# Node degrees and first edges of a graph kernel: a search in the sorted target list in place of one-hot counts

## The reference

```
x = x + attention_gnn(layernorm(x), edge_attr, src, dst, ...)   # softmax over the edges of one target
x = x + gated_experts(layernorm(x), ...)
x = x + mean_gnn(layernorm(x), src, dst, ...)                   # sums / max(degree, 1)
x = x + routed_experts(layernorm(x), ...)

# in attention_gnn:
ft = (feat @ W_fc).reshape(N, 8, 32);  eh, et = <ft, attn_h>, <ft, attn_t>     # per node and head
ee = <(edge_attr @ W_e), attn_e>                                               # per edge and head
e = leaky_relu(eh[src] + ee + et[dst])
a = softmax of e over the edges with the same dst
rst = segment_sum(ft[src] * a, dst)
```

## Time and profile before

| | us |
|---|---|
| three runs, median (lowest to highest) | 3279.69 (3274.05 to 3285.43) |
| the profiled execution | 3277.21 |
| its span | 3275.7 |
| PE busy | 2385.6 (73%) |
| DVE busy | 1885.0 (58%) |
| POOL busy | 1795.3 (55%) |
| ACT busy | 1315.9 (40%) |

### The profile page before, as it was taken

The page is one execution under the profiler, slowest core; times in us unless marked ns, Lnnn a source line. Parts: engine busy times, 40 slices in busy tenths (PEclk is TensorE's granted clock), DMA queues, the critical chain, the costliest instruction groups (busy, mean ns, idle before and its releaser), DMA issues. The chain is left out here.

```text
span 3275.7 us, 49346 instructions
## 1 busy us (share of the span) xinstructions
PE 2385.6 (73%) x12682; PEld 1986.9 (61%) x12682; DVE 1885.0 (58%) x5767; ACT 1315.9 (40%) x4659; POOL 1795.3 (55%) x1886
## 2 busy tenths in 40 slices
PE   5995366667666665657899698888888888746088
PEld 4884256666666565446677576666666666635077
DVE  7981388888889887657455433333333333366245
ACT  2332255555555544523445333333333333355033
POOL 0007777777777777041000677777777777250645
PEclk9998778887888877778999656656565566757589
DMA  7336644444444445460000333333333333321342
GB/s 209 100 109 149 201 110 112 113 112 112 112 111 114 112 112 153 139 185 26 23 16 19 113 106 105 107 105 106 105 106 105 106 105 106 113 62 34 97 139 86
DMA packets 264113, 348.42 MB, mean 106 GB/s; under 512 B 153632, under 2 KB 193686, under 8 KB 262331
## 3 DMA queue, kind: packets, MB, share of 16 engines
q0 software_dynamic: 87936, 235.05, 25.3%
q1 hardware_dynamic: 175908, 110.32, 13.1%
HBM read 288.25 MB, written 61.20 MB: 107 GB/s over the span
## 5 line engine op out<-in xcount | busy, mean ns | idle before, releaser
L1384 POOL DMA_INDIRECT Gb<-normed_rows,SRCT x784 | 741.3, 946 | 519.6 <-SPq L1376 281.0
L1405 PE MATMUL pAb<-HOTb,Gb 128*128 128x128 f32 x3136 | 845.5, 426 | 149.4 <-DMA Gb<-normed_rows,SRCT 117.5
L1405 PEld LDWEIGHTS pAb<-HOTb,Gb 128*128 128x128 f32 x3136 | 659.6, 297 | 335.4 <-DMA Gb<-normed_rows,SRCT 274.7
L1445 DVE TENSOR_TENSOR ACC<-ACC,pAb 128x256 f32 x784 | 330.8, 422 | 641.8 <-PE pAb L1405 569.1
L975 POOL DMA_INDIRECT GX<-ft_rows,SRCT x432 | 413.3, 957 | 131.8 <-issue 128.6
L1064 ACT ACTIVATE ACC<-apA 128x254 f32 x784 | 300.4, 383 | 413.5 <-PE apA L1137 339.4
L1137 PE MATMUL apA<-AHOT,GX 128*128 128x129 f32 x1920 | 306.2, 330 | 81.1 <-DVE GX L1286 80.8
L1137 PEld LDWEIGHTS apA<-AHOT,GX 128*128 128x128 f32 x1920 | 292.2, 243 | 98.8 <-DVE GX L1286 98.6
L1424 ACT ACTIVATE HOTb<-OFFb 128x1024 f32<-128x1024 f32 x98 | 103.6, 1057 | 604.8 <-PE pAb L1405 604.7
L975 POOL DMA_INDIRECT G<-ft_rows,SRCT x288 | 273.8, 951 | 87.6 <-issue 87.1
L1420 ACT ACTIVATE OFFb<-iota,NRELb 128x128 f32<-128x128 f32 x784 | 239.6, 388 | 6.7
(11 more groups left out here) (381 smaller groups left out, 4182.4 us busy)
## 6 DMA issues: line engine op xcount, KB each, us to landing
ebuf<-in_edge_attr_dram SPq DMA_DIRECT2D x49, 448.0 KB
Gb<-normed_rows,SRCT POOLq DMA_INDIRECT x784, 2.7
rows_by_expert<-ffn_PADT SPq DMA_DIRECT2D x1, 10360.0 KB, 42.3
sT<-rows_by_expert SPq DMA_DIRECT2D x80, 129.5 KB, 2.1
GX<-ft_rows,SRCT POOLq DMA_INDIRECT x480
sums_by_rank<-rrowa SPq DMA_DIRECT2D x49, 128.0 KB, 1.7
sums_by_rank<-rrowb SPq DMA_DIRECT2D x49, 128.0 KB, 1.7
GX<-in_x_dram SPq DMA_DIRECT2D x11, 560.0 KB
```

What stands on the lines that cost most here:

```text
L1384: pool.indirect_dma_start(G[g % R][m][:, :], None, TABLE[:, :], bass.IndirectOffsetOnAxis(ap=SRCT[:, t:t + 1], axis=0)).then_inc(g_in[g % ...
L1405: last = nc.tensor.matmul(pA[b][:, o:o + EP], G[k][m][:, c * 128:(c + 1) * 128], HOT[k % 2][:, m, :], start=True, stop=True)
L1445: last = nc.vector.tensor_tensor(acc[:, :, ds(b, EP)], acc[:, :, ds(b, EP)], pA[q][:, o:o + KD * EP].rearrange("p (c r) -> p c r", c=KD), ...
```

## The change

Instead of counting all edges, the new kernel searches. `dst` is cut into 3,125 rows of 32 edges, and 25 rows belong to each of 125 partitions (800 edges, the segment). For each of the 6,251 numbers v = 50p + i (one more than the nodes) it seeks the first edge whose target is not below v.

- First level: with the first target of each segment (`SX`) and of the next one (`SNX`), `segment_hits` marks on VectorE for each v the one segment in which it falls, in four batches of 13, 13, 13 and 12 values of i. `segments` multiplies each 125 x 125 mark matrix on TensorE with `SEG`, whose columns hold the first targets of the 25 rows of each segment and the number of its first row. `segment_rows` counts the rows that start below v and so finds v's row.
- Second level: GpSimd gathers for each i the row of 32 targets of all p, 51 indirect DMAs of 128 rows with 128 bytes, and `first_edges` counts the targets below v. The first edge is 32 times the row plus that count, and a degree is the difference of two neighbours.

The batches stand in groups 1 to 4 of the loop (hits up to two batches ahead); the four passes over all targets at the start, the `count` blocks, the transposition and the scan and prefix of degrees are gone. The last steps move: the cast `DX` goes behind the loop, `FIRSTI` no longer needs the prefix product, `CONT` is built after the last projection, and SP issues edge blocks 46 to 48 ahead of the load of `F`, which now also waits for `rq_ready`. SP gets three more DMAs at the start, GpSimd five more short instructions. The core of the diff:

```diff
-        HS = 4
-        FB = F[:, :].bitcast(bf16)
-        hotA = [...]
+        NV = NT + 1
+        SB = 13
+        SW = [min(SB, NV - b * SB) for b in range((NV + SB - 1) // SB)]
+        BW = 32
+        BK = E // BW // P
...
@@ sync
                 load_x(0)
+                ds32 = dst.rearrange("(p j) -> p j", j=BK * BW)
+                for a in PARTS:
+                    sp.dma_start(DVI[a, :], ds32[a, :]).then_inc(dv_in, 16)
+                sp.dma_start(SNI[0:P - 1, :], ds32[1:P, 0:1], allow_slow_non_contiguous=True).then_inc(dv_in, 16)
...
-                for c in range(n + 3, NCH - 3):
+                for c in range(n + 3, NCH):
                     load(c)
+                sp.wait_ge(rq_ready, 1)
                 sp.wait_ge(st, 16 * NT)
                 sp.dma_start(F[:, :], STARTD.rearrange("(p j) h -> p (j h)", j=ES)).then_inc(f_in, 16)
-                for c in range(NCH - 3, NCH):
-                    load(c)
@@ gpsimd
                 nc.gpsimd.memset(ETS[:, :], 0.0).then_inc(ets_zero, 1)
+                nc.gpsimd.memset(SEG[:, :], 0.0).then_inc(node_set, 1)
+                nc.gpsimd.iota(NODE.rearrange("p (i q) -> p i q", q=P), pattern=[[1, SB], [NT, P]], ...)
+                nc.gpsimd.iota(NODEV[:, :], pattern=[[1, NV]], base=0, channel_multiplier=NT, ...)
+                nc.gpsimd.memset(ROWI[:, :], 0).then_inc(node_set, 1)
+                nc.gpsimd.iota(SEG[:, BK:BK + 1], pattern=[[0, 1]], base=0, channel_multiplier=BK, ...)
                 nc.gpsimd.memset(V[:, :], 0.0).then_inc(v_zero, 1)
+                pool.wait_ge(rows_ready, 1)
+                dw = dst.rearrange("(r k) -> r k", k=BW)
+                for i in range(NV):
+                    pool.indirect_dma_start(WORDS[:, i * BW:(i + 1) * BW], None, dw,
+                                            bass.IndirectOffsetOnAxis(ap=ROWI[:, i:i + 1], axis=0)).then_inc(words_in, 16)
                 pool.wait_ge(etd_out, 16)
@@ tensor
-                def count(c):
-                    pe.wait_ge(hot, c + 1)
-                    for m in range(C):
-                        last = nc.tensor.matmul(pH[0:NT, 0:P], hotB[c % HS][:, m, :], hotA[c % HS][:, m, :], ...)
+                def segments(b):
+                    pe.wait_ge(oh_ready, b + 1)
+                    if b:
+                        pe.wait_ge(seg_read, b)
+                    for i in range(SW[b]):
+                        o = i * (BK + 1)
+                        last = nc.tensor.matmul(pH[0:P, o:o + 128], OH[b % 2][:, i * P:(i + 1) * P], SEG[:, :], start=True, stop=True)
+                    last.then_inc(seg_found, 1)
...
                     turn_edges(g)
-                    count(2 * g)
+                    if 1 <= g <= len(SW):
+                        segments(g - 1)
                     if g + 1 < NGR:
                         turn(g + 1)
-                    if 2 * g + 1 < NCH:
-                        count(2 * g + 1)
                     score(g)
                     project(g)
@@ vector
+                def segment_hits(b):
+                    if b >= 2:
+                        dve.wait_ge(seg_found, b - 1)
+                    w = SW[b] * P
+                    nc.vector.tensor_scalar(OH[b % 2][:, 0:w], NODE[:, 0:w], SNX[:, b:b + 1], None, ALU.is_le)
+                    dve.drain()
+                    nc.vector.scalar_tensor_tensor(OH[b % 2][:, 0:w], NODE[:, 0:w], SX[:, b:b + 1], OH[b % 2][:, 0:w], ALU.is_gt,
+                                                   ALU.mult).then_inc(oh_ready, 1)
+                def segment_rows(b):
+                    dve.wait_ge(seg_found, b + 1)
+                    ...
+                    nc.vector.tensor_tensor(lt, v[:, :, 0:BK], NODEV[:, a].unsqueeze(2).to_broadcast([P, w, BK]), ALU.is_lt)
+                    nc.vector.tensor_copy(ROWF[:, a], v[:, :, BK]).then_inc(seg_read, 1)
+                    nc.vector.tensor_reduce(LESS[:, a], lt, AX.X, ALU.add)
+                    ...
+                def first_edges():
+                    dve.wait_ge(words_in, 16 * NV)
+                    nc.vector.tensor_copy(WORDF, WORDS[0:P, :])
+                    v = WORDF.rearrange("p (i k) -> p i k", k=BW)
+                    nc.vector.tensor_tensor(v, v, NODEV[:, :].unsqueeze(2).to_broadcast([P, NV, BW]), ALU.is_lt)
+                    nc.vector.tensor_reduce(LESS[:, :], v, AX.X, ALU.add)
+                    nc.vector.scalar_tensor_tensor(ROWF[:, :], ROWF[:, :], float(BW), LESS[:, :], ALU.mult, ALU.add)
+                    nc.vector.tensor_tensor(DEG[:, :], ROWF[:, 1:NV], ROWF[:, 0:NT], ALU.subtract)
...
+                segment_bounds()
+                segment_hits(0)
                 norm(1)
                 stats(1)
+                segment_hits(1)
                 for g in range(NGR):
...
-                    for c in range(2 * g + 2, min(2 * g + 4, NCH)):
-                        onehots(c)
+                    if 1 <= g <= len(SW):
+                        segment_rows(g - 1)
+                        if g + 1 < len(SW):
+                            segment_hits(g + 1)
                     if g + 3 < NGR and chunk_of(g + 3) > chunk_of(g + 2):
                         stats(chunk_of(g + 3))
+                dve.wait_ge(ld, 96)
+                nc.vector.tensor_copy(DX[:, :], DXI[:, :])
...
+                first_edges()
...
+                nc.vector.tensor_tensor(FIRSTI[0:P, :], ROWF[:, 0:NT], UN[:, :], ALU.add).then_inc(first_ready, 1)
+                dve.wait_ge(f_ready, NGR)
+                nc.vector.tensor_tensor(CONT[:, :], DX[:, 1:ES + 1], DX[:, 0:ES], ALU.is_equal)
```

More of the change, by code:

```diff
@@ L318, in front @@
         eT = [sb(s, f"eT{k}", [128, C // 2 * EP]) for k in range(2)]
-        HS = 4
-        FB = F[:, :].bitcast(bf16)
-        hotA = [FB[:, k * C * P:(k + 1) * C * P].rearrange("p (c a) -> p c a", a=P) for k in range(HS)]
-        hotB = [FB[:, HS * C * P + k * C * NT:HS * C * P + (k + 1) * C * NT].rearrange("p (c b) -> p c b", b=NT)
-                for k in range(HS)]
+        NV = NT + 1
[3 more added lines that the diff above has]
+        BK = E // BW // P
+        HITS = SB * P
+        NODE = F[0:P, 0:HITS]
+        OH = [F[0:P, (1 + k) * HITS:(2 + k) * HITS] for k in range(2)]
+        WORDS = F[:, HITS:HITS + NV * BW].bitcast(i32)
+        WORDF = F[0:P, HITS + NV * BW:HITS + 2 * NV * BW]
+        LT = F[0:P, 3 * HITS:3 * HITS + SB * BK]
+        DVI = F[0:P, 3 * HITS + SB * BK:3 * HITS + SB * BK + BK * BW].bitcast(i32)
+        SNI = sb(s, "SNI", [P, 1], i32)
+        SX = sb(s, "SX", [P, len(SW)])
+        SNX = sb(s, "SNX", [P, len(SW)])
+        SEG = sb(s, "SEG", [P, 128])
+        NODEV = sb(s, "NODEV", [P, NV])
+        ROWF = sb(s, "ROWF", [P, NV])
+        LESS = sb(s, "LESS", [P, NV])
+        ROWI = sb(s, "ROWI", [128, NV], i32)
         QI = sb(s, "QI", [QB, NQ, EP], i32)
         QF = sb(s, "QF", [QB, NQ, EP])
-        DA = sb(s, "DA", [EP, ES])
         DB = sb(s, "DB", [EP, ES])
@@ L370, in front @@
         sc_ready, v_ready = sem("edge_scores"), sem("edge_scores_kept")
[L371 to L373 removed]
+        dv_in, node_set = sem("dst_segments_in"), sem("node_numbers_set")
+        oh_ready, seg_found, seg_read = sem("segment_onehots"), sem("segments_found"), sem("segments_read")
+        rows_ready, words_in = sem("dst_rows_known"), sem.gather("dst_rows_in")[0]
+        tot, pre, first_ready = sem("node_totals"), sem("node_prefix"), sem("firsts_ready")
         etd_out, cont_ready, cont_out, cq_in = sem("et_out"), sem("cont_ready"), sem("cont_out"), sem("cont_by_tile")
@@ L577, in _ @@
                     turn_edges(g)
-                    count(2 * g)
+                    if 1 <= g <= len(SW):
+                        segments(g - 1)
                     if g + 1 < NGR:
                         turn(g + 1)
-                    if 2 * g + 1 < NCH:
-                        count(2 * g + 1)
                     score(g)
                     project(g)
-                nc.tensor.matmul(pH[0:NT, 0:P], ZB[:, 0:NT], ZB[:, 0:P], start=False, stop=True,
-                                 skip_group_check=True).then_inc(counted, 1)
                 turn_edges(NGR)
-                pe.wait_ge(dt_ready, 1)
-                nc.tensor.transpose(pQ[0:P, 0:NT], DT[:, :], ident[0:NT, 0:NT]).then_inc(deg_ready, 1)
+                pe.wait_ge(tot, 1)
+                nc.tensor.matmul(pQ[0:P, 64:65], below[0:P, 0:P], TOT[:, :], start=True, stop=True).then_inc(pre, 1)
                 score(NGR)
                 turn_edges(NGR + 1)
[L594 to L597, removed]
                 score(NGR + 1)
@@ L683, in _, with segment_bounds @@
                 nc.vector.memset(UN[:, :], 1.0)
[L685 to L692, removed]
+                def segment_bounds():
+                    dve.wait_ge(dv_in, 48)
+                    dve.wait_ge(node_set, 5)
+                    nc.vector.tensor_copy(SEG[:, 0:BK], DVI[:, 0:BK * BW:BW])
+                    nc.vector.tensor_copy(SX[:, 0:1], DVI[:, 0:1])
```

(13 more changed lines are left out.)

62 lines of the change are left out of this document (34 added, 28 removed).

## The result

The changed kernel takes 3240.86 us, median of four runs (3239.67 to 3242.96), where the kernel before takes 3277.07 (3274.05 to 3285.43): a ratio of 0.9886, 95% interval 0.9866 to 0.9907. That is 36.2 us or 1.1% less. The profiled execution took 3240.99, its span is 3239.3. The prediction said 3241.

The account below looks back on a forecast made before the run. The loop, with PE and DVE nearly full, sets when GpSimd may begin; 126.7 + 2.6 + 3.3 + 1.5 = 134.1 against 173.6 saves 39.5, less 2 at the start: 37.5, so 3241 us, range 3231 to 3255.

Parts of the forecast that it names:

- The plain group: Loop: a group without counts takes 5.76 us instead of 7.32, so 22 groups take 126.7 us.
- The segment products: TensorE, g = 1 to 4: 51 added products, 1.45 us a group, +3.3 us in the counted stretch.
- late statistics: Loop, g = 2: segment work on VectorE ahead of `stats` delays ScalarE's `root`, +1.5 us (bounds 0 and 9).
- `root`: ScalarE in the loop: without late statistics it costs only itself, about 0.32 us in 8 groups, +2.6 us.
- PE's bare work: Loop: PE's group without the two counts (2.06 us) is 5.26 us, below the floor of 5.76.
- The start: Three added SP DMAs, 0.4 MB, delay the end of ScalarE's stall at `keep(0)`: +2 us (0 to 5).
- POOL: GpSimd beside the loop: 51 word gathers take 65 to 102 us, cost nothing, margin 25 to 62 us.
- The end of the block: Behind the loop: moved loads leave SP 15 us of wait, costing nothing; rival: `F` path ends the block, 3246, chance 0.04.
- More: Rival, loop and start: `root` and segment work hide wholly, zeros not delayed; 47 us saved, 3231, chance 0.10.
- Half: Rival, loop: stores and loads or late statistics pace groups at about 6.5 us; 16 lost, 3257, chance 0.12.
- the search isn't hidden: Rival, GpSimd: late rows or slow gathers delay the scatters; wholly in line 27 us slower, 3305, chance 0.03.
- The clock: Rival, loop: PE's stops in every group lower its clock, groups 9.4 us, 79 us more, 3320, chance 0.03.

Follow-up runs that it names:

- e5: Changed kernel with each of the 51 target rows gathered twice: 3255.00 us, ratio 0.9940 to the kernel before.
- e7: Changed kernel with the next group's edge block turned ahead of project and copied ahead of the stores of rows: 3221.38 us, ratio 0.9839.
- e10: Changed kernel with 49 idle count blocks put back on TensorE, VectorE left free: 3276.28 us, ratio 1.0007 to the kernel before.
- e1: Changed kernel with 49 idle count blocks put back on TensorE, on a chip with disturbed traces: 3825.51 us, ratio 1.018 to the kernel before there.
- e6: Changed kernel with loads of edge blocks 46 to 48 put back behind the load of `F`: 3242.02 us.
- e12: Changed kernel with one idle pair of one-hots a group on VectorE, no counts, on a disturbed chip: 3756.33 us, ratio 1.0004 to the kernel before there.
- e8: Kernel before with the edge block of the next group turned ahead of project and copied ahead of the rows: 3274.16 us, ratio 0.9993.
- e11: Changed kernel with two idle pairs of one-hots a group put back on VectorE, no counts on TensorE: 3285.78 us, ratio 1.0031.

## Why the prediction was right

**The chain.** Loop end, `ETD`, `C0`, scatters, gathers: the order held. e5 is the counter-test: once the search was later than `C0`, the next phase came later by what the scatters were late (12.0 and 11.2), and the median grew by 14.1.

**The number.** That 3241 is met to 0.1 us is luck. It was taken between 3239.7 and 3242.2, and the saving by medians is 36.2 where 37.5 was forecast.

**The loop.** 134.1 forecast, 134.33 measured. The form of the group was right, but this closeness too is in part luck: the sum hides terms that were off and cancelled.
- The plain group: 5.76 forecast, 5.76 measured, from the last group of the old loop. e7 shows that this floor was ScalarE's order, e10 that PE's floor with counts is 7.25.
- The segment products were mis-sized: 1.45 us a batch forecast, 2.84 measured (58.13 to 60.97). I had taken the x16 of score for 16 products; they are records, and score has 8 products. Each fp32 product leaves two in these traces, each transposition one (x4 for the four of `turn`). 13 products are 26 records at 0.11 us.
- Groups 2 to 4 took 7.76, 8.23 and 7.54, 6.2 over plain, where I had 4.8 (3.3 for PE, 1.5 for late statistics). PE stands ahead of score only in the second of them, for 0.43 us; that is what ScalarE's wait of 2.2 us for the statistics and its `root` cost, the rest fell where ScalarE had to wait for PE's products anyway. The other 5.8 are the products (2.84, 2.84 and 2.63), of which PE's wait of 0.81 hides a part. So PE's term was 2.5 too small, that of the statistics 1.1 too large.
- `root` costs 0.18 in each of the other seven groups instead of 0.32 in eight: 1.3 instead of 2.6.
- PE's bare work, 5.26 forecast, is 4.92 (e7). The 1.19 of the edges included 0.16 of issue ahead of `count`; in the changed kernel they take 0.99, in e7's order 0.87. It changed nothing here, since ScalarE's floor stood above it, but PE's wait is 0.81 in each plain group and not 0.5.

**The start.** +2 forecast, +2.6 at `keep(0)`, +2.0 at the third group (57.14 against 55.13). That it fits so well is no proof: in the other runs with the same DMAs at the start (e1 to e6, e10 to e12) `keep(0)` runs at 47.55 to 49.41, and in e8, with those of the kernel before, at 48.16. By these the term is between nothing and 2.6.

**The scatters.** They began 38.4 us earlier and not 37.5. `C0` began 36.8 us earlier (205.16 for 241.91) and took 0.94 us instead of 2.58. I had not looked at what ran beside it (last section).

**POOL.** 51 gathers of 128 bytes a row took 0.95 + 0.30 each, 64 us, just under the range of 65 to 102. The price does not follow the bytes: the attention gathers, with rows of 264 fp32 numbers, take 0.96. The high end is real too: in e11, beside one-hots, the same 51 took 91.9 us busy and 15.2 of issue, 107, a little over my bound.

**The end of the block.** 15 us of SP's wait forecast, 16.9 measured, and e6 gives 12.4 us as the price of the moved loads (12 forecast).

**The rivals.** *More* failed, since the segment products did cost some 6 us. *Half* failed; the loop is paced by neither loads nor stores, which ran at 170 GB/s in e7's faster loop against 142 here. *The end of the block* failed with 16.9 us left, and *the search isn't hidden* with the gathers over at 143. *The clock* failed: it is 1.00 in the loop although PE stops 0.81 us in each plain group. The rule of the Trainium skill, "TensorE: Matmul & The Clock Gate", section "A second HAM failure mode: psum-queue depth-cycling", by which frequent short stops of PE make the clock swing, is not borne out by this loop. Among these loops the clock is clearly lower only where the stops are longer: 0.90 in e11, with stops of 4.2 to 5.8 us.

## What to carry to other kernels

Where two engines are both nearly full in a loop, a change that relieves only one of them can show nothing (e10, e11); find the floor of each engine and of each fixed order, and compare only the largest before and after. After such a change the new floor is often an order written for the old balance, and swapping two steps, worth nothing to be seen before (e8), was worth 19.5 us after it (e7). A forecast that comes out to the microsecond still wants its terms checked one by one; here three were off. When a duration is read from a group of records, check first how many records one product leaves.

## What the runs showed of the hardware

GpSimd's indirect DMAs can be slowed by what VectorE does at the same time: word gathers, scatters and row gathers alike. In e11, from 50 to 240 us, the word gathers take 1.80 us in the mean instead of 0.95; here one beside two pairs of one-hots (x4), of three that start beside them, of which the first took 0.94 and the second 1.85:

```profile
L523 POOL DMA_INDIRECT F<-in_dst_dram,ROWI x51 | 91.9, 1801 | 90.7 <-DVE ROWI L748 75.5 <-issue 15.2
```

```profile
89.88 6.25 DVE L768 TENSOR_TENSOR CONTU<-iota 128x2000 bf16<-128x2000 f32 x4
...
93.30 2.75 POOL L523 DMA_INDIRECT F<-in_dst_dram,ROWI  x1 [0.30 <-issue]
```

A scan does so too. In e6 the row gather that starts 0.1 us behind the first of eight scans takes 2.50 us, the next ones beside them 1.44. In e5 one scatter starts in the middle of a scan of 784 columns and takes 1.43 us, its neighbours 0.99 and 0.97:

```profile
218.93 0.99 POOL L533 DMA_INDIRECT et_at_starts<-ETS,FIRSTI  x1 [0.31 <-issue]
219.09 1.79 DVE L862 TENSOR_TENSOR_SCAN DB<-ONE,DB 128x784 f32<-128x784 f32 x1
220.22 1.43 POOL L533 DMA_INDIRECT et_at_starts<-ETS,FIRSTI  x1 [0.30 <-issue]
```

The same scan ran from 241.77 to 243.56 beside the kernel before's `C0` of 2.58 us and was over before the changed kernel's. e8, the kernel before in another order, had it over at 241.90, ahead of its `C0`, and only a short VectorE pass beside that:

```profile
242.23 1.37 POOL L497 DMA_INDIRECT C<-et_rows,DXI  x1 [233.98 <-DMA et_rows<-ETS]
```

So the scan explains most of the 1.6 us by position; no run tests it alone. The Trainium skill, "SBUF — State Buffer", section "Who interferes with whom", says that a VectorE instruction with two inputs in SBUF contends with GpSimd instructions that read SBUF: the rows agree, if the indirect DMA reads its row numbers from SBUF, where the kernel keeps them. It also infers that tensor_tensor does not hinder the generation of descriptors; the 2.75 us beside it show that an indirect DMA is hindered all the same, and no run tells whether at its row numbers or at its descriptors.
